# A fused time-mix, channel-mix and mixture-of-experts kernel: rank counts one step later, output projection moved, third norm and a plus-one on ScalarE

## Chip, cores and metric

One core of one Trainium2 chip. The metric is device time in microseconds of one launch, everything from the first to the last instruction; the times shown are the median of three launches.

## What is computed

The input x is 8 x 1024 tokens of 256 numbers (8192 tokens), all in float32. Cut to what matters:

```python
xn = layernorm(x)                                    # norm without gain
y  = layernorm(xn; ln1)                              # first norm of the block
r, w, k, v = sigmoid(y Wr), -exp(y Ww), y Wk, y Wv
num_t = decay*num + exp(w+k)*v;  den_t = decay*den + exp(w+k)   # scan over the 1024 tokens
xn = xn + (r * num/den) Wo
z  = layernorm(xn; ln2)
xn = xn + sigmoid(z Wrec) * (relu(z Wkey)**2) Wval   # 256 -> 1024 -> 256
x  = x + xn
h  = layernorm(x)                                    # third norm
gate = sigmoid(h Sel);  top 4 of 32 experts per token
out = x + sum over the 4 of  gate_e * relu(h K_e) V_e
```

## The kernel before

The kernel has three stages, one behind the other. The **mix stage** does everything up to the choice of experts, writes the new x to DRAM (`residual`), and scatters each token's normed row to the lists of its four experts. The **expert stage** works through 160 blocks of 256 list rows. The **combine stage** adds the four weighted expert rows to x. The change is wholly in the mix stage (`mix_phase`), so the rest is not described.

Every float32 matmul that must be exact is done as three matmuls of type fp32r on a high and a low part of both operands: high x high, high x low, low x high. So whatever goes into a matmul is first copied to a `_hi` tile (ScalarE, L588, L637, L653, L699) and then has its rest taken into a `_lo` tile (VectorE, L739, L835, L859, L912).

**Tiles and steps.** The tokens are cut in NT = 16 tiles of 512 (J = 4 subtiles of 128). There are 19 steps. In step t the engines work at the same time on tile t (time mix: projections, scan, output projection), on tile U = t-1 (channel mix) and on tile V = t-2 (third norm, routing); the scatter of rows is for tile W = t-3. Each engine has its own written-out order of work within a step, the function `step` in its block, and the engines meet only in semaphores. So a wait holds back everything behind it on the same engine. `run` (L304) unrolls the first steps, loops over pairs of steps, and unrolls the last ones.

**TensorE's order in one step**, with the lines: eight groups of six projection matmuls of tile t, m = 0 to 7 (L385), where before m = 6 come the eight transposes of the second norm of U (L375, `second_transposes`, wait for `xn2_ready` and `xn2_last_ready`); keys 0 to 3 of U, six matmuls each (L385, wait for `xn2t_ready` and `ku_ready`); the eight transposes of the third norm of V (L375, wait for `x3_ready`); keys 4 to 7; the recurrence gate of U: per subtile one bias matmul (L496, `ones_rows` times `rec_bias`, of which only two of the 64 rows, 0 and 32, are not zero) and six more (L499 to L501); the routing logits of V (L516); the transposes of the first norm of tile t+1 (L375, `t1`); 96 value matmuls of U (L535 to L539, wait for `klo_ready`); the rank counts of V, 14 small bf16 matmuls on `mask` (L554, L557); 24 matmuls of the output projection of t (L570 to L572, wait for `y_ready`).

**ScalarE's order**: u and th_r of tile t (L621, L625), second norm of U applied (L594, `xn2`, three subtiles; VectorE does the fourth, L821), the exponentials `den` (L632, wait for `ku_ready`), `xn2t_hi` (L637), then the eight keys: relu(0), relu(1), square(0), relu(2), square(1), relu(3), square(2), relu(4), x3t copies (L668), relu(5), relu(6), square(3), relu(7), square(4), first norm of t+1 applied (L594), squares 5 to 7, `th_c` (L685), `eg` (L692), `xn1t_hi` (L588), `y_hi` (L699). A square is two instructions (L652, L653).

**VectorE's order**: `xp` of U from the output projection (L800, wait for `o_ready`), statistics of the second norm (L727, L733), `th_c` and `xp` of V (L813, L817), fourth subtile of the second norm (L821), u (L827, gives `ku_ready`), statistics of the third norm, `xn2t_lo` (L835), `num` (L843), third norm of V applied (L849, gives `x3_ready`, waits for the scale from GpSimd, L1079), four scans (L868), statistics of the first norm of t+1, reciprocals and `k_lo` in turns, `xn1t_lo` (L739), routing of V (`route`: L940 adds one, L942 reciprocal, top four, `mask` at L968), `y_lo` (L912), and `route_slots`: L974 to L986, with a wait for the rank counts, and a wait for GpSimd's product L1168 (`chosen` times `place`) in the middle.

**GpSimd's order**: scale of the second norm (L1073 to L1079), x added to xp (L1141, waits for both parts of xn2), two scatters (L1124), scale of the third norm, `u` from `den` (L1148), two scatters, scale of the first norm of t+1, six scatters, `th_r` times `u` (L1158), six scatters, `chosen` times `place` (L1168). **SP** only loads x and stores xp.

Of the kernel before, what the change touches and what calls it, by code (L numbers as in the profile page):

```python
# [23 lines left out]
ALU = mybir.AluOpType  # L24
# [3 lines left out]
P = 128  # L28
# [7 lines left out]
NT = N // TILE  # L36
# [85 lines left out]
def mix_phase(nc, mix, sem, g):  # L122
# [30 lines left out]
    LO_ROW, BIAS_ROWS = 32, 64  # L153
# [119 lines left out]
    over_done, area_cleared = per("over_done area_cleared")  # L273
# [53 lines left out]
    with nc.Block() as block:  # L327
# [44 lines left out]
        def _(pe):  # L372
# [24 lines left out]
            def step(t, p, pair):  # L397
                has_t, has_u, has_v, has_next, _ = stages(t)
                U, V = t - 1, t - 2
# [21 lines left out]
                if has_t:  # L421


                    for m in range(8):
# [5 lines left out]
                        elif m in (2, 3):  # L430
                            pe.wait_ge(u_ready, 2 * t + m - 1)
# [9 lines left out]
                elif has_u:  # L441
                    second_transposes()
# [99 lines left out]
                if has_v:  # L542

                    pe.wait_ge(mask_ready, V + 1)
                    if has_next:
                        pe.wait_ge(xn1t_ready, 2 * t + 4)
                    elif has_u:
                        pe.wait_ge(xn2t_ready, 2 * U + 2)
                    else:
                        pe.wait_ge(rank_used, V)  # L550
                    for j in range(J + 1):
                        cols = ps[:, TR, j * E:(j + 1) * E]
                        for i in range(j):
                            mm = pe.matmul(cols, ones_bf[:], mask[:, i, :], start=i == 0,  # L554
                                           stop=j == J and i == j - 1)
                        if j < J:
                            mm = pe.matmul(cols, tri_bf[:], mask[:, j, :], start=j == 0, stop=True)  # L557
                    mm.then_inc(rank_ready, 1)
# [25 lines left out]
        def _(act):  # L584
# [5 lines left out]
            def ln_apply(n, dst, src, tile, ready, subtiles=J):  # L590

                act.wait_ge(rs_ready[n], tile + 1)
                for j in range(subtiles):
                    ins = act.activation(dst[:, j, :], src[:, j, :], ACT.Identity, scale=rs[:, n, j:j + 1],  # L594
# [3 lines left out]
            def step(t, p, pair):  # L598
# [64 lines left out]
                square(2)  # L663
                relu(4)
# [24 lines left out]
                if has_v:  # L689
# [3 lines left out]
                                   scale=-1.0).then_inc(eg_ready, 1)  # L693
# [25 lines left out]
        def _(dve):  # L719
# [39 lines left out]
            def step(t, p, pair):  # L759
                has_t, has_u, has_v, has_next, _ = stages(t)  # L760
                U, V = t - 1, t - 2
# [33 lines left out]
                if has_u:  # L795

                    dve.wait_ge(o_ready, U + 1)
                    landed(dve, x1_stored, p, pair, 3)
# [690 lines left out]
```

## Time and profile before

| what | value |
|---|---|
| median of three runs | 1458.73 us (1451.87 to 1459.62) |
| span of the profiled execution | 1618.1 us |
| busy: TensorE, VectorE, ScalarE, GpSimd | 1184.4, 1096.5, 678.8, 889.3 us |
| mean granted clock of TensorE | 0.862 of full speed |
| mix stage in the profile | 0 to about 880 us |

The page of the profile gives the profiled execution by its span, 1618.1 us, and has no other time for it; it is 159 us above the median of the runs that were timed without a profile. In the steady part of the mix stage (100 to 800 us) one step takes about 50 us, the granted clock is 0.97 to 1.00, and nothing in DMA is near its limit. A row of a timeline reads: start in us from the start of the span, duration in us, engine, line, operation, output and inputs, shapes, count, and in brackets how long the engine had been idle before it and what ended that.

### The profile page before, as it was taken

What the parts mean: (1) busy time and instruction counts of PE and PEld (TensorE: products, weight loads), DVE (VectorE), ACT (ScalarE), POOL (GpSimd) and SP (SyncE); (2) the same over time, 40 slices, a digit from 0 to 9 for tenths busy, and PEclk for the clock granted to TensorE, in tenths of its full rate; (3) what the DMA queues carried; (4) which work ended last, traced back from release to release, by engine and by line L of the source; (5) the groups of instructions that cost most, each with busy time, mean ns of one, the idle gap of its engine ahead of it and who ended that gap; (6) DMA issues with size and microseconds to landing.
All of it is one profiled execution on the core that took longest, in us unless ns stands there. A gap on an engine that the chain in (4) does not pass through costs nothing. (4 is left out here: it accounts for less than half of the span.)

```text
span 1618.1 us, 28319 instructions
## 1 busy us (share of the span) xinstructions
PE 1184.4 (73%) x7399; PEld 1058.3 (65%) x7400; DVE 1096.5 (68%) x2519; ACT 678.8 (42%) x1265; POOL 889.3 (55%) x967
## 2 busy tenths in 40 slices
PE   6799999999999999999881266766776766773000
PEld 5688887888878887788771266666766666673000
DVE  4889898888988889888847444444544444443987
ACT  2555565445654456444443143443443443442000
POOL 1634676666766677667657455555555555554000
PEclk9899999999999999999985588798788788886555
DMA  5000121111111121121163754445444444434998
GB/s 184 14 27 13 68 70 60 66 53 69 65 59 65 46 78 59 61 70 60 54 274 143 249 151 137 140 137 149 133 146 144 133 143 142 141 113 158 390 390 321
DMA packets 101917, 201.25 MB, mean 124 GB/s; under 512 B 16983, under 2 KB 49901, under 8 KB 100464
## 3 DMA queue, kind: packets, MB, share of 16 engines
q1 hardware_dynamic: 63216, 120.34, 23.6%
q0 software_dynamic: 27648, 67.70, 11.5%
q10 hardware_dynamic: 11008, 12.65, 2.2%
q8 instruction: 22, 0.36, 0.1%
q14 instruction: 23, 0.19, 0.0%
HBM read 105.28 MB, written 103.71 MB: 129 GB/s over the span
## 5 line engine op out<-in xcount | busy, mean ns | idle before, releaser
L1359 POOL DMA_INDIRECT expert_rows<-y,dest x320 | 320.4, 1001 | 257.1 <-issue 224.9
L1124 POOL DMA_INDIRECT lists<-rows,slot x256 | 276.5, 1080 | 73.3 <-issue 70.4
L1269 PE MATMUL ps<-xt_hi,keys 128*128 128x256 f32 x640 | 180.0, 341 | 114.0 <-issue 110.1
L1336 DVE TENSOR_TENSOR xt_lo<-ps,xt_hi 128x512 fp32r<-128x512 f32 x160 | 110.5, 690 | 186.0 <-ACT xt_hi L1296 107.6
L1269 PEld LDWEIGHTS ps<-xt_hi,keys 128*128 128x128 f32 x640 | 131.4, 226 | 130.7 <-issue 129.5
L1308 ACT ACTIVATE y<-ps 128x512 f32<-128x512 f32 x160 | 96.1, 601 | 130.2 <-PE ps L1284 113.2
L535 PE MATMUL ps<-wv_hi,k_hi 128*128 128x256 f32 x512 | 149.6, 292 | 0.0
L537 PE MATMUL ps<-wv_lo,k_hi 128*128 128x256 f32 x512 | 147.8, 289 | 0.9 <-issue 0.9
L539 PE MATMUL ps<-wv_hi,k_lo 128*128 128x256 f32 x512 | 147.6, 288 | 0.3 <-issue 0.3
L1296 ACT ACTIVATE xt_hi<-ps 128x512 fp32r<-128x512 f32 x160 | 96.6, 604 | 122.0 <-PE ps L1256 101.9
L1282 PE MATMUL ps<-experts_w,h_hi 128*128 x320 | 108.4, 339 | 47.6 <-DVE h_lo L1343 36.7
L1256 PE MATMUL ps<-consts,xr 128*128 128x128 f32 x640 | 115.3, 311 | 32.7 <-DMA xr<-lists 32.7
L1343 DVE SCALAR_TENSOR_TENSOR h_lo<-ps,h_hi 128x256 fp32r<-128x256 f32 x160 | 67.9, 424 | 93.5 <-ACT h_hi L1302 68.4
L644 ACT ACTIVATE kr<-ps,bias_k 128x512 f32<-128x512 f32 x128 | 88.2, 689 | 73.0 <-PE ps L385 70.0
L1302 ACT ACTIVATE h_hi<-ps 128x256 fp32r<-128x256 f32 x160 | 62.3, 389 | 125.6 <-PE ps L1269 87.1
L1256 PEld LDWEIGHTS ps<-consts,xr 128*128 128x128 f32 x640 | 89.2, 162 | 33.4 <-DMA xr<-lists 33.4
L1282 PEld LDWEIGHTS ps<-experts_w,h_hi 128*128 128x128 f32 x320 | 73.6, 230 | 55.6 <-issue 55.6
L385 PE MATMUL ps<-xn2t_hi,wk_hi 128*128 128x512 f32 x256 | 104.0, 406 | 1.4 <-DVE xn2t_lo L835 1.4
L385 PE MATMUL ps<-xn1t_hi,wt_hi 128*128 128x512 f32 x256 | 102.3, 400 | 2.6 <-DVE xn1t_lo L739 2.6
L1283 PE MATMUL ps<-experts_w,h_hi 128*128 x320 | 103.3, 323 | 0.0
L1284 PE MATMUL ps<-experts_w,h_lo 128*128 x320 | 102.3, 320 | 0.0
L385 PE MATMUL ps<-xn2t_lo,wk_hi 128*128 128x512 f32 x256 | 102.0, 398 | 0.0
(201 smaller groups left out, 3544.4 us busy)
## 6 DMA issues: line engine op xcount, KB each, us to landing
xr<-lists SPq DMA_DIRECT2D x160, 260.0 KB
ye<-expert_rows SPq DMA_DIRECT2D x32, 1024.0 KB, 8.1
x_sb<-in_x SPq DMA_DIRECT2D x16, 512.0 KB, 3.8
residual<-xp SPq DMA_DIRECT2D x16, 512.0 KB, 4.9
experts_raw<-in_expert_in SPq DMA_DIRECT2D x8, 1024.0 KB, 15.1
lists<-zeros SPq DMA_DIRECT2D x25, 260.0 KB, 10.8
expert_rows<-y,dest POOLq DMA_INDIRECT x320
resid<-residual SPq DMA_DIRECT2D x20, 256.0 KB, 5.4
```

Of the source, the lines that this page charges most:

```text
L385: mm = pe.matmul(bank, w(k), m(k), start=n == 0, stop=n == last)
L535: pe.matmul(bank, k_hi[:, f, c], wv_hi[:, f, :], start=f == 0 and j % 2 == 0, stop=False, skip_group_check=True)
L537: pe.matmul(bank, k_hi[:, f, c], wv_lo[:, f, :], start=False, stop=False, skip_group_check=True)
L539: mm = pe.matmul(bank, k_lo[:, f, c], wv_hi[:, f, :], start=False, stop=f == KF - 1, skip_group_check=True)
L1124: pool.indirect_dma_start(lists, bass.IndirectOffsetOnAxis(ap=slot[:, q, n:n + 1], axis=0), rows[:, q, n // TOPK, :], None).then_inc(scatt ...
L1256: mm = pe.transpose(ps[:, XT + r % 2, k * BLOCK + s * P:k * BLOCK + (s + 1) * P], xr[:, r % SLOTS, s, k * P:(k + 1) * P], ident)
L1269: mm = pe.matmul(ps[:, H + q, 0:BLOCK], keys[:, (r - 1) % SLOTS, half, k * DE:(k + 1) * DE], m[:, q, k, :], start=n == 0, stop=n == 3 * KD ...
L1282: pe.matmul(cols, h_hi[:, q, c], v_hi, start=True, stop=False)
L1283: pe.matmul(cols, h_hi[:, q, c], v_lo, start=False, stop=False)
L1284: mm = pe.matmul(cols, h_lo[:, q, c], v_hi, start=False, stop=True)
L1336: dve.tensor_tensor(xt_lo[:, q].rearrange("p k b -> p (k b)"), ps[:, XT + q, :], xt_hi[:, q].rearrange("p k b -> p (k b)").bitcast(F32), A ...
L1359: pool.indirect_dma_start(expert_rows, bass.IndirectOffsetOnAxis(ap=dest[:, r, s:s + 1], axis=0), y[:, r, s, :], None, bounds_check=OUT_RO ...
```

## The change

Four edits in the mix stage, all in the written-out orders:

1. **Rank counts a step later.** TensorE's 14 small matmuls for a tile are no longer behind the value matmuls of step t but in step t+1, between projection groups m = 1 and m = 2 (`ranks`, for tile W = t-3). On VectorE `route_slots` is cut in two: `route_places` (the old L974, L978) behind the statistics of the second norm, and the rest (the old L983, L986) behind the fourth subtile of the second norm, ahead of L827. GpSimd's product (the old L1168) moves from the end of a step to behind the scale of the second norm, ahead of L1141.
2. **Output projection straight behind the value matmuls**, which follows from 1. On VectorE `y_lo` now comes ahead of `route`.
3. **The bias matmul of 128 rows** in place of 64: `BIAS_ROWS = P`; rows other than 0 and 32 are zero as before.
4. **Third norm and plus one on ScalarE.** The four `tensor_scalar` of L849 become four activations with scale and bias, placed between square(2) and relu(4); the plus one of L940 becomes an activation behind `eg`, with a wait for it. In addition `route` waits for the scatter of the tile before last, and GpSimd waits for the last `x3_ready` before it writes the next scale.

`run` unrolls six first steps in place of four. TensorE's place for the third norm's transposes (between key 3 and key 4) is not changed.

```diff
-    LO_ROW, BIAS_ROWS = 32, 64
+    LO_ROW, BIAS_ROWS = 32, P
...
-        for t in range(4):
+        for t in range(6):
...
-        with eng.Fori(2, NT // 2 - 1) as pair:
+        with eng.Fori(3, NT // 2 - 1) as pair:
...
+                def ranks():
+                    if not has_w:
+                        return
+                    pe.wait_ge(mask_ready, W + 1)
+                    if not has_t:
+                        pe.wait_ge(xn2t_ready, 2 * min(t - 1, NT))
+                        pe.wait_ge(rank_used, W)
+                    for j in range(J + 1):
...
+                    mm.then_inc(rank_ready, 1)
...
                         elif m in (2, 3):
+                            if m == 2:
+                                ranks()
                             pe.wait_ge(u_ready, 2 * t + m - 1)
...
-                if has_v:
-
-                    pe.wait_ge(mask_ready, V + 1)
...
-                    mm.then_inc(rank_ready, 1)
...
                 square(2)
+                if has_v:
+                    landed(act, scattered, p, pair, 4, J * TOPK)
+                    ln_apply(2, rows[:, p], xp[:, p], V, x3_ready)
                 relu(4)
...
-                                   scale=-1.0).then_inc(eg_ready, 1)
+                                   scale=-1.0).then_inc(eg_exp, 1)
+                    act.wait_ge(eg_exp, V + 1)
+                    act.activation(eg[:], eg[:], ACT.Identity, bias=ones_f[:, 0:1]).then_inc(eg_ready, 1)
...
                     ln_aggr(1, U)
+                if has_w:
+                    route_places(W)
...
                                       rs[:, 1, J - 1:J], ALU.subtract, ALU.mult).then_inc(xn2_last_ready, 1)
+                if has_w:
+                    route_slots(p, pair, W)
                 if has_t:
                     for m in range(KD):
                         dve.wait_ge(u_ready, 2 * t + m + 1)
...
-                if has_v:
-                    landed(dve, scattered, p, pair, 4, J * TOPK)
-                    dve.wait_ge(rs_ready[2], V + 1)
-                    for j in range(J):
-                        ins = dve.tensor_scalar(rows[:, p, j, 0:D], xp[:, p, j, :], mv[:, 2, j, 0:1],
-                                                rs[:, 2, j:j + 1], ALU.subtract, ALU.mult)
-                    ins.then_inc(x3_ready, 1)
...
-                dve.tensor_scalar(eg[:], eg[:], 1.0, None, ALU.add).then_inc(route_step, 1)
...
+            def route_slots(p, pair, W):
+
+                dve.wait_ge(placed_ready, W + 1)
                 dve.tensor_reduce(slot_f[:], chosen[:], AX_X, ALU.add).then_inc(place_summed, 1)
-                dve.wait_ge(place_summed, V + 1)
-                landed(dve, scattered, p, pair, 4, J * TOPK)
-                dve.tensor_copy(slot[:, p, :], slot_f[:]).then_inc(slot_ready, 1)
+                dve.wait_ge(place_summed, W + 1)
+                landed(dve, scattered, p, pair, 5, J * TOPK)
+                dve.tensor_copy(slot[:, 1 - p, :], slot_f[:]).then_inc(slot_ready, 1)
...
+                if has_w:
+                    pool.wait_ge(place_ready, W + 1)
...
+                                       ALU.mult).then_inc(placed_ready, 1)
+                if has_u:
                     pool.wait_ge(xn2_ready, U + 1)
                     pool.wait_ge(xn2_last_ready, U + 1)
                     pool.tensor_tensor(xp[:, 1 - p], xp[:, 1 - p], x_sb[:, 1 - p], ALU.add).then_inc(xx_ready, 1)
                 scatter(t, 1 - p, 0, 2)
                 if has_v:
+                    if not isinstance(V, int) or V > 0:
+                        settled_on(pool, x3_ready, V)
                     ln_scale(2, V)
```

## Rows read from the trace of the kernel before

**Rows 1.** Waits of TensorE, 100 to 800 us: total us, times, longest
```profile
PE ps L375 <- ACT xn L594: 23.1, 22, 2.0
PE ps L570 <- DVE y_lo L912: 4.4, 7, 0.7
PE ps L557 <- DVE mask L968: 3.0, 6, 0.9
```

**Rows 2.** TensorE timeline, the step that begins at 401.18
```profile
401.18 0.40 PE L385 MATMUL ps<-xn1t_hi,wt_hi 128*128 128x512 f32 x1
...
410.30 1.09 PE L375 MATMUL ps<-consts,xn 128*128 128x128 f32 x8 [0.79 <-ACT xn L594]
...
414.00 0.40 PE L385 MATMUL ps<-xn2t_hi,wk_hi 128*128 128x512 f32 x1
...
419.60 1.03 PE L375 MATMUL ps<-consts,rows 128*128 128x128 f32 x8
...
426.16 0.38 PE L496 MATMUL ps<-rec_bias,ones_rows 64*128 64x256 f32 x1
...
427.37 0.38 PE L496 MATMUL ps<-rec_bias,ones_rows 64*128 64x256 f32 x1
...
433.71 1.06 PE L375 MATMUL ps<-consts,xn 128*128 128x128 f32 x8 [0.93 <-ACT xn L594]
```

**Rows 3.** TensorE timeline, the end of that step and the first matmul of the next
```profile
447.62 0.19 PE L557 MATMUL ps<-mask,tri_bf 128*128 128x32 bf16 x1
...
447.98 0.36 PE L570 MATMUL ps<-wo_hi,y_hi 128*128 128x256 f32 x1
...
452.56 0.40 PE L385 MATMUL ps<-xn1t_hi,wt_hi 128*128 128x512 f32 x1
```

**Rows 4.** ScalarE timeline, same step
```profile
421.34 0.63 ACT L653 ACTIVATE k_hi<-kr 128x512 fp32r<-128x512 f32 x1
...
431.38 2.08 ACT L594 ACTIVATE xn<-x_sb,shift_n,rs 128x256 f32<-128x256 f32 x4 [0.64 <-POOL shift_n L1107]
```

**Rows 5.** VectorE timeline, the end of that step and the start of the next
```profile
439.43 2.30 DVE L940 TENSOR_SCALAR eg<-eg 128x128 f32<-128x128 f32 x1
...
452.25 0.69 DVE L983 TENSOR_REDUCE slot_f<-chosen 128x16 f32<-128x512 f32 x1 [1.18 <-POOL chosen L1168]
...
453.09 1.66 DVE L800 SCALAR_TENSOR_TENSOR xp<-xn,ratio,ps 128x256 f32<-128x256 f32 x4
...
456.29 0.38 DVE L733 BATCH_NORM_AGGREGATE mv<-stats 128x2 f32<-128x6 f32 x4
...
457.94 1.23 DVE L817 TENSOR_TENSOR xp<-xp,th_c 128x1024 f32<-128x1024 f32 x1
...
460.94 0.69 DVE L827 TENSOR_TENSOR u<-ps,u 128x512 f32<-128x512 f32 x1 [0.67 <-PE ps L385]
...
462.91 1.29 DVE L835 TENSOR_TENSOR xn2t_lo<-ps,xn2t_hi 128x512 fp32r<-128x512 f32 x2
```

**Rows 6.** VectorE timeline, third norm in the next step
```profile
467.79 1.38 DVE L849 TENSOR_SCALAR rows<-xp,mv,rs 128x256 f32<-128x256 f32 x4 [2.01 <-POOL shift_n L1079]
```

**Rows 7.** GpSimd timeline, same stretch
```profile
439.08 2.55 POOL L1158 TENSOR_TENSOR th_r<-th_r,u 128x512 f32<-128x512 f32 x2
...
450.93 1.29 POOL L1168 TENSOR_TENSOR chosen<-chosen,place 128x512 f32<-128x512 f32 x1 [1.67 <-DVE place L974]
...
458.38 0.85 POOL L1079 TENSOR_TENSOR shift_n<-minus_mean,rs 128x4 f32<-128x4 f32 x1
460.93 2.39 POOL L1141 TENSOR_TENSOR xp<-xp,x_sb 128x1024 f32<-128x1024 f32 x1 [1.70 <-ACT xn L594]
```

**Rows 8.** VectorE timeline, the drain
```profile
840.74 0.23 DVE L940 TENSOR_SCALAR eg<-eg 128x128 f32<-128x128 f32 x1 [4.41 <-ACT eg L692]
```

**Rows 9.** TensorE timeline, the drain, after its last matmul at 803.44
```profile
812.41 1.97 PE L375 MATMUL ps<-consts,xn 128*128 128x128 f32 x8 [8.69 <-ACT xn L594]
```

**Rows 10.** Windows of 2 us: PE, PEld, DVE, ACT, POOL busy, PEclk, DMA
```profile
806.00:808.00 2.00, 0.00 (x0) 0.00 (x0) 1.93 (x8) 0.00 (x0) 0.00 (x0) 0.70 0.00 0
```

More of the change, by code:

```diff
@@ L397, in step @@
             def step(t, p, pair):
-                has_t, has_u, has_v, has_next, _ = stages(t)
-                U, V = t - 1, t - 2
+                has_t, has_u, has_v, has_next, has_w = stages(t)
+                U, V, W = t - 1, t - 2, t - 3
+                def ranks():
[6 more added lines that the diff above has]
+                    for j in range(J + 1):
+                        cols = ps[:, TR, j * E:(j + 1) * E]
+                        for i in range(j):
+                            mm = pe.matmul(cols, ones_bf[:], mask[:, i, :], start=i == 0,
+                                           stop=j == J and i == j - 1)
+                        if j < J:
+                            mm = pe.matmul(cols, tri_bf[:], mask[:, j, :], start=j == 0, stop=True)
+                    mm.then_inc(rank_ready, 1)
                 def second_transposes():
@@ L440, in step @@
                                (lambda k: xn1t_hi[:, k, :], lambda k: xn1t_lo[:, k, :]), KD, proj_ready)
-                elif has_u:
+                else:
+                    ranks()
                     second_transposes()
@@ L541, in step @@
                     mm.then_inc(val_ready, 1)
-                if has_v:
-                    pe.wait_ge(mask_ready, V + 1)
[L545 to L557, printed above, removed]
-                    mm.then_inc(rank_ready, 1)
                 if has_t:
@@ L798, in step @@
                     landed(dve, x1_stored, p, pair, 3)
+                    after(dve, x3_ready, U - 1)
                     for j in range(J):
@@ L906, in step @@
                     lo1(t + 1)
-                if has_v:
-                    route(t, p, pair, V)
                 if has_t:
@@ L929, in step, with route @@
                 if has_v:
-                    route_slots(t, p, pair, V)
-            RS = 7
-            def route(t, p, pair, V):
+                    route(p, pair, V)
+            RS = 6
+            def route(p, pair, V):
                 def after_route(n):
@@ L1137, in step @@
                         split(2, wv_hi, wv_lo, raw_v)
+                if has_w:
+                    pool.wait_ge(place_ready, W + 1)
+                    if isinstance(W, int) and W == NT - 1:
+                        pool.wait_ge(over_done, 1)
+                    pool.tensor_tensor(chosen[:].rearrange("p (j k) e -> p j k e", j=J),
+                                       chosen[:].rearrange("p (j k) e -> p j k e", j=J),
+                                       place[:].unsqueeze(2).broadcast_to([P, J, TOPK, E]),
+                                       ALU.mult).then_inc(placed_ready, 1)
+                if has_u:
                     pool.wait_ge(xn2_ready, U + 1)
@@ L1162, in step @@
                     split(0, wk_hi, wk_lo, raw_k)
-                if has_v:
-                    pool.wait_ge(place_ready, V + 1)
-                    if isinstance(t, int) and V == NT - 1:
-                        pool.wait_ge(over_done, 1)
-                    pool.tensor_tensor(chosen[:].rearrange("p (j k) e -> p j k e", j=J),
-                                       chosen[:].rearrange("p (j k) e -> p j k e", j=J),
-                                       place[:].unsqueeze(2).broadcast_to([P, J, TOPK, E]),
-                                       ALU.mult).then_inc(placed_ready, 1)
             run(pool, step)
```

37 lines of the change are left out of this document (18 added, 19 removed).

## The prediction

> **What bounds the kernel now.** I read the page first: its slices show TensorE near full in the mix stage, VectorE close behind, and DMA low. A busy share does not say who sets the pace, so next came the waits of TensorE over the steady part [rows 1]. There are 14 steps in these 700 us, and the longest entry is 23.1 us in all, 1.65 us a step. The rest is work in TensorE's own queue: it is the bound, and what lengthens or shortens that queue shows in the end nearly one for one. Then I laid out one step along TensorE's timeline [rows 2, 3]. The step begins at 401.18 (s), the second norm's transposes start at 410.30 after an idle 0.79, key 0 starts at 414.00 (K), the third norm's transposes at 419.60, the gate at 426.16, the first norm's transposes at 433.71 after an idle 0.93, the rank counts at 447.62, the output projection at 447.98, and the next step begins at 452.56: 51.4 us. All that follows asks two things of the other engines' timelines [rows 4 to 7]: when, counted from s or from K, do they hand TensorE what it waits for, and is that later than TensorE gets there?
>
> Two averages. The 0.93 recurs in each step, so of the 23.1 us about 13.0 are the first norm's and 10.1, or 0.72 a step, the second norm's. From s to K is 12.82 us here; with the mean wait in place of 0.79 it is 12.75.
>
> **Third norm on ScalarE, the largest term.** VectorE now does it in 1.38 us after a wait of 2.01 [rows 6], before key 3 is through, so TensorE goes into the transposes without idling [rows 2]. Moved, it stands on ScalarE behind square(2), whose last instruction starts at 421.34 and takes 0.63, so ScalarE is free at 421.97 [rows 4]. ScalarE has been busy without a gap since relu(1), so nothing lets it come sooner. Four activations with scale and bias of just this shape take 2.08 [rows 4], so the normed rows are there at about 424.0, and TensorE, which has not moved the transposes, has wanted them since 419.60. It stands for 4.4 us, and keys 4 to 7 stand behind it. Both ends of this count from K, so a later K doesn't soften it. **+4.4 us a step.** relu(4) is queued behind the four activations, but its key comes later than they do. The wait that this edit adds for an old scatter is met long before. What VectorE gives up, 1.38 plus the 2.01, is free, since VectorE isn't what TensorE waits for afterwards: credit zero.
>
> **Routing pieces ahead of key 0.** VectorE starts `xp` at 453.09, s + 0.53, and ends the statistics at 456.67, s + 4.1 [rows 5]. Now two small additions follow; the same size of operation took 0.23 with nothing in its way [rows 8], so 0.5 together, an estimate. `th_c` and the addition to `xp` (1.27, then 1.23, rows 5) end at s + 7.1. GpSimd's scale was held up by that addition: 0.85 for four elements, ending with it [rows 5, 7]. Its product of `chosen`, 1.29 [rows 7], also reads two tiles of SBUF, so I let it start at 7.1 and end at 8.5. VectorE waits for it, then reduces (0.69, rows 5) to about 9.3. Then comes the cast of the slots. Meanwhile GpSimd has gone on to add x to `xp`, 2.39 us [rows 7], from about 8.9 to 11.3. Does that hold the cast up? No row has a cast against it. Below, it costs nothing: reduction and cast together took 0.84 (452.25 to 453.09, rows 5). Above, the nearest row is the plus one: from float32 SBUF to SBUF, 0.23 in the drain and 2.30 in the steady step, where it ended at 441.73, just after GpSimd's products ended at 441.63 [rows 5, 7, 8]. I take it as held, until s + 11.45; free, it would be s + 9.45. A gain is excluded, as the cast is new at this place.
>
> The Trainium skill, page "SBUF — State Buffer", section "Who interferes with whom", says that copy, cast and tensor_scalar can run in a mode that takes the port pair which VectorE shares with GpSimd, for a whole instruction. By that rule the cast is held and the sum is the 1513 below; if casts of 16 elements stayed out of that mode, it would be the 1485. The trace agrees on tensor_scalar (2.30 against 0.23) and shows no cast in this position.
>
> Behind the cast stand the two subtractions of L827, 1.38 [rows 5], which before were through at 461.63. From there to the end of `xn2t_lo` at 464.20 is 2.57: ScalarE does the two exponentials first and only then the high copies. So key 0 can start at s + 11.45 + 1.38 + 2.57 = s + 15.4. TensorE gets there at s + 12.3 (12.03 without a wait, plus 0.36 for the rank counts, rows 3, now in this stretch). Against the 12.75 of before: **+2.65 us a step**; with a free cast, +0.65.
>
> **What is given back.** The bias matmul of 64 rows starts a group of seven that takes 1.21 us (426.16 to 427.37, rows 2). 24 matmuls of 512 columns took 5.60 (414.00 to 419.60), so one of 256 is worth 0.117 and seven are 0.82. I take the excess of 0.39 as the price of changing between 64 and 128 rows: four times, **-1.5 us**. At worst the excess is not from the rows and nothing is gained. The first norm's transposes, whose wait was 0.93, come 5.5 us later against K while ScalarE's application of that norm hangs on work that is no more than 2 us later: **-0.93**. The rank counts leave the end: **-0.36**; with them go the waits for the mask and `y_lo`, 7.4 us in 14 steps [rows 1], since `y_lo` is no longer behind the routing: **-0.5**. The plus one costs ScalarE some 0.3 ahead of `xn1t_hi`, which TensorE wants only a stretch of 96 value matmuls later: zero. Its 2.30 on VectorE is slack, zero. If that cover were gone it would be a gain of 2, since VectorE would have been the bound. The last tile's counts, lists and plan keep their chain, and the two more unrolled steps run the same instructions: zero.
>
> **The sum.** 4.4 + 2.65 - 1.5 - 0.93 - 0.36 - 0.5 = +3.8 us a step for the 13 steps with all four tiles in flight (3 to 15), 49 us. Step 2 has the third norm but no counts, +1.5; step 16 has no projections, and the norm, slots and bias come to about +5; step 1 only saves its bias, -1.5. Together +54. The profiled execution's span of 1618.1 would become 1672. It lies 159 us above the median, and the page doesn't say in which stage, so I carry the 54 over as microseconds: 1458.7 + 54 = **1513**.
>
> **Rivals.**
> *The cast is not held up* (for: it is 16 elements and could slip in; against: the 2.30). 14 steps lose 2.0 less each: 1485.
> *The clock falls in the new idle time.* In the drain TensorE's last matmul began at 803.44, and in the window from 806 to 808 the granted clock was already 0.70, so the engine was going to its lower level of 1.2 GHz; eight transposes then took 1.97 instead of 1.03 [rows 2, 9, 10]. Whether an idle 4.4 us does the same no row shows. If it happens each time, the transposes lose 0.94 and a key group of 1.40 costs another 1.4, 2.3 us in each of 15 steps: 1548. If in half of them, 1530. Against it: idle 0.79 and 0.93 are no measure. The Trainium skill, page "TensorE: Matmul & The Clock Gate", section "HAM oscillation — how this bites in real kernels", tells of such an alternation; the drain agrees, and by it the sum would be the 1548.
> *Faster: the end of the step gives way.* The 24 output matmuls took 4.58 us (447.98 to 452.56) for 24 x 0.117 = 2.8, and the 96 value matmuls took from about 434.5, where the transposes of 433.71 are through, to 447.6, 13.1 for 11.2. If these 3.7 us a step are only TensorE being fed late, by VectorE's full queue, then freeing VectorE gives them back, and with a free cast the step is 3.8 - 2.0 - 3.7 = 1.9 shorter: 1432. It decides where the two new waits together stay under 7.0 - 1.9 = 5.1 us a step. For it: VectorE waits little, and the change relieves it of most. Against: the waits listed for TensorE there are 0.5 us a step, and the 4.4 alone nearly fills the 5.1.
> *It cancels*: a part of that give-back, or a third norm that comes 2 us earlier than laid out, leaves it within 0.5%.
>
> **Numbers.** The case laid out, 0.50 (its own range 1500 to 1530, with the clock falling now and then); free cast 0.20; clock falling in most steps 0.17; faster 0.08; cancelled 0.05. A measurement of this kernel tells about 0.5%, 7 us, from no change, which gives faster 0.08, same 0.05, slower 0.87. The range from 1478 to 1548 takes in the first three but for the outer half of the clock case.
>
> **What would show it.** In the changed kernel: TensorE's wait for ScalarE's rows in front of the third norm's transposes, 4.4 us in 15 steps (the decisive row; were it under 2, the forecast falls). A wait of some 3 us for `xn2t_lo` in front of key 0, and the slots' cast taking about 2 us instead of 0.17. The gap from one bias matmul to the next, 0.82 instead of 1.21. No wait for the first norm's transposes, for `y_lo` or the mask. The step at about 55 us instead of 51.4.

## The result, and the profile after

The changed kernel takes 1537.06 us (median of four runs, 1534.25 to 1542.48), the kernel before on the same chip 1457.06 us (1451.87 to 1459.62). The ratio is 1.0573, with a 95% interval of 1.0547 to 1.0599: **slower by 80 us**. The forecast was 1513, in a range of 1478 to 1548.

The profiled execution of the changed kernel took 1536.0 us. The first part of its page:

```profile
span 1534.1 us, 28169 instructions
...
PE 1119.5 (73%) x7399; PEld 1005.3 (66%) x7400; DVE 1112.2 (72%) x2439; ACT 718.4 (47%) x1345; POOL 911.2 (59%) x967
```

This span can't be set against the 1618.1 of before as it stands, because the chips differ in speed. On two of the chips used later the kernel before takes about 1620 us, on the third 1453, and its first profile has a span like the slower ones. What differs most is the expert stage, which the change doesn't touch; so profiles are compared up to the first load of that stage, and times only within a chip. To that load the kernel before took 915.6 us (the "about 880" of the table ahead of the prediction stops short of it) and the changed one 977.7.

One step of the changed kernel on TensorE's timeline, the same places as in [rows 2, 3] (start, duration, engine, line, operation, in brackets the idle time before it and what ended it):

```profile
530.86 0.40 PE L385 MATMUL ps<-xn1t_hi,wt_hi 128*128 128x512 f32 x1
...
539.59 1.09 PE L375 MATMUL ps<-consts,xn 128*128 128x128 f32 x8
...
545.84 0.50 PE L385 MATMUL ps<-xn2t_hi,wk_hi 128*128 128x512 f32 x1 [2.40 <-DVE xn2t_lo L847]
...
557.46 1.97 PE L375 MATMUL ps<-consts,rows 128*128 128x128 f32 x8 [4.21 <-ACT rows L596]
...
566.78 0.28 PE L515 MATMUL ps<-rec_bias,ones_rows 128*128 128x256 f32 x1
...
567.60 0.28 PE L515 MATMUL ps<-rec_bias,ones_rows 128*128 128x256 f32 x1
...
571.77 1.07 PE L375 MATMUL ps<-consts,xn 128*128 128x128 f32 x8
...
587.07 0.40 PE L385 MATMUL ps<-xn1t_hi,wt_hi 128*128 128x512 f32 x1
```

Key 0 waits 2.40 us for `xn2t_lo`, the third norm's transposes wait 4.21 us for ScalarE's `rows`, and after that they take 1.97 us instead of 1.03. The two bias matmuls stand 0.82 apart instead of 1.21. The first norm's transposes no longer wait. The step is 56.2 us long. TensorE's waits of the changed kernel from 200 to 750 us (total, times, longest) hold nothing else; before, [rows 1], neither of the two was among them:

```profile
PE ps L375 <- ACT rows L596: 42.1, 10, 4.2
PE ps L385 <- DVE xn2t_lo L847: 23.6, 10, 2.4
```

ScalarE's timeline of the same step, to be read beside [rows 4]:

```profile
554.82 0.62 ACT L655 ACTIVATE k_hi<-kr 128x512 fp32r<-128x512 f32 x1
555.34 2.06 ACT L596 ACTIVATE rows<-xp,shift_n,rs 128x256 f32<-128x256 f32 x4
```

The normed rows are finished at 557.40, and TensorE starts at 557.46. VectorE's timeline, to be read beside [rows 5]:

```profile
537.95 1.35 DVE L831 TENSOR_SCALAR xn<-xp,mv,rs 128x256 f32<-128x256 f32 x1
539.22 0.67 DVE L988 TENSOR_REDUCE slot_f<-chosen 128x16 f32<-128x512 f32 x1
540.03 2.00 DVE L991 CAST slot<-slot_f 128x16 uint32<-128x16 f32 x1
541.94 1.28 DVE L839 TENSOR_TENSOR u<-ps,u 128x512 f32<-128x512 f32 x2
...
544.50 1.29 DVE L847 TENSOR_TENSOR xn2t_lo<-ps,xn2t_hi 128x512 fp32r<-128x512 f32 x2
```

and GpSimd's, beside [rows 7]:

```profile
537.87 1.28 POOL L1147 TENSOR_TENSOR chosen<-chosen,place 128x512 f32<-128x512 f32 x1
539.61 2.38 POOL L1154 TENSOR_TENSOR xp<-xp,x_sb 128x1024 f32<-128x1024 f32 x1 [0.46 <-ACT xn L596]
```

The 16 elements of the cast take 2.00 us, and the cast ends as GpSimd's addition to `xp` ends at 541.99. The addition had begun first.

The table lays out every kernel in the same way. It is worked out from TensorE's timelines and is the mean over the eleven steps 4 to 14, in us: from the step's start (s) to the second norm's transposes (T2), key 0, the third norm's transposes (T3), the gate, the logits, the first norm's transposes (T1), the value matmuls (V), the output projection (O), and the next step.

| kernel | step | s to T2 | to key 0 | to T3 | to gate | to logits | to T1 | to V | to O | to next |
|---|---|---|---|---|---|---|---|---|---|---|
| before | 50.86 | 9.33 | 3.69 | 5.60 | 6.56 | 4.76 | 2.79 | 1.02 | 13.27 | 3.85 |
| after | 54.42 | 8.67 | 6.16 | 10.92 | 8.38 | 3.28 | 1.70 | 0.82 | 11.60 | 2.88 |
| third norm back (e1) | 50.59 | 9.38 | 6.23 | 6.24 | 6.46 | 3.28 | 2.83 | 1.10 | 12.17 | 2.88 |
| third norm only (e2) | 52.83 | 8.24 | 3.69 | 9.97 | 8.71 | 4.76 | 1.70 | 0.83 | 11.96 | 2.95 |
| bias only (e3) | 50.99 | 9.03 | 3.70 | 5.60 | 6.46 | 3.28 | 4.35 | 1.32 | 13.30 | 3.95 |
| after again (e4) | 54.34 | 8.68 | 6.16 | 10.21 | 9.00 | 3.28 | 1.70 | 0.83 | 11.60 | 2.88 |
| filler (e5) | 52.36 | 8.68 | 6.16 | 10.71 | 6.53 | 3.28 | 1.70 | 0.83 | 11.59 | 2.88 |
| slots late (e6) | 51.14 | 8.68 | 3.66 | 10.30 | 8.21 | 3.28 | 1.70 | 0.83 | 11.59 | 2.88 |
| T3 behind key 5 (e7) | 50.23 | 8.68 | 6.16 | 11.19 | 3.91 | 3.29 | 1.70 | 0.83 | 11.60 | 2.88 |
| both repairs (e9) | 48.85 | 10.01 | 3.85 | 10.28 | 4.16 | 3.29 | 1.94 | 0.83 | 11.62 | 2.88 |
| both, norm earlier (e10) | 48.43 | 9.00 | 3.69 | 10.29 | 5.03 | 3.28 | 1.70 | 0.82 | 11.72 | 2.88 |
| norm back, slots late (e11) | 49.34 | 8.78 | 3.68 | 5.61 | 6.46 | 3.28 | 4.22 | 1.41 | 13.02 | 2.88 |

(For e7, e9 and e10 the stretch to T3 holds two keys more and that to the gate two fewer. For before, e2 and e3 the stretch from V to O also holds the 14 rank counts, 0.36 us.) From the start of step 2 to the end of step 14 the changed kernel loses 47.9 us (654.9 against 702.8), and in what is left of the mix stage 14.4. That is 62 us; the other 18 of the 80 are probably a matter of the chips, which the experiments come to.

### The profile page after: what moved, and what is told of

Same layout as the page of the kernel before. It is cut to its first block and busy times, and to the rows that moved or that the text cites. A ratio compares the mean times of both kernels' runs of the same rounds, so it can differ in the third digit from the quotient of the medians.

```text
span 1534.1 us, 28169 instructions
## 1 busy us (share of the span) xinstructions
PE 1119.5 (73%) x7399; PEld 1005.3 (66%) x7400; DVE 1112.2 (72%) x2439; ACT 718.4 (47%) x1345; POOL 911.2 (59%) x967
## 5 line engine op out<-in xcount | busy, mean ns | idle before, releaser
L1274 PE MATMUL ps<-xt_hi,keys 128*128 128x256 f32 x640 | 156.4, 307 | 78.3 <-DVE keys L1332 55.3
L864 DVE TENSOR_TENSOR k_lo<-ksq,k_hi 128x512 fp32r<-128x512 f32 x128 | 113.7, 935 | 111.1 <-ACT k_hi L655 111.1
L1274 PEld LDWEIGHTS ps<-xt_hi,keys 128*128 128x128 f32 x640 | 112.4, 194 | 100.1 <-DVE keys L1332 78.0
L385 PE MATMUL ps<-xn2t_hi,wk_hi 128*128 128x512 f32 x256 | 118.1, 461 | 33.2 <-DVE xn2t_lo L847 33.2
L1261 PE MATMUL ps<-consts,xr 128*128 128x128 f32 x640 | 98.8, 278 | 33.8 <-DMA xr<-lists 33.8
L385 PE MATMUL ps<-xn2t_hi,wk_lo 128*128 128x512 f32 x256 | 111.4, 435 | 0.0
L1332 DVE CAST keys<-experts_w 128x512 fp32r x160 | 75.1, 469 | 40.3 <-issue 37.4
L623 ACT ACTIVATE u<-ps,bias_t 128x512 f32<-128x512 f32 x32 | 22.1, 690 | 169.0 <-PE ps L385 169.0
L385 PE MATMUL ps<-xn1t_lo,wt_hi 128*128 128x512 f32 x256 | 101.0, 395 | 0.0
L385 PE MATMUL ps<-xn1t_hi,wt_lo 128*128 128x512 f32 x256 | 100.6, 393 | 0.0
```

The source lines that it names most:

```text
L385: mm = pe.matmul(bank, w(k), m(k), start=n == 0, stop=n == last)
L864: dve.tensor_tensor(k_lo[:, m, :], ksq[:, m % KRING, :], k_hi[:, m, :].bitcast(F32), ALU.subtract).then_inc(klo_ready, 1)
L1261: mm = pe.transpose(ps[:, XT + r % 2, k * BLOCK + s * P:k * BLOCK + (s + 1) * P], xr[:, r % SLOTS, s, k * P:(k + 1) * P], ident)
L1274: mm = pe.matmul(ps[:, H + q, 0:BLOCK], keys[:, (r - 1) % SLOTS, half, k * DE:(k + 1) * DE], m[:, q, k, :], start=n == 0, stop=n == 3 * KD ...
```

## The experiments

Twelve runs. e0 to e3 ran on one of the slower chips, e4 to e7 on the faster, e8 to e11 on another slower one. Each ratio is to the kernel before on the same chip.

### The kernel before and the changed kernel again (e0, e8, e4)

The kernels unchanged, one run of before at the head of each of two sets, and the changed kernel in the third.

> The kernel before unchanged, for a second profile: the profile on record lies 159 us above its median. If that was an execution with a slow expert stage, the mix stage ends at 916 us again (first load of list rows) and the span is about 1457; if the profile itself stretches this kernel, the span is 1618 again.

> The kernel before once more, for a profile where it takes about 1455 us: the profiles so far are from a chip on which it takes 1618. If only the expert stage differs between the chips, the mix stage ends at 915 us here too, and the expert stage takes about 415 us; if the chips differ in the mix stage, it ends near 898 us and the expert stage takes 430 us, as behind the changed kernel.

> The changed kernel unchanged, next to the kernel before on the same chip. In the two profiles on record its mix stage ends 62 us later (977.7 against 915.6), while its median lies 80 us higher. If the mix stage is all, the difference here is 62 us; if the expert stage also takes longer because of the change, it is 80 us again, and the first load of list rows still starts at 978.

Measured: e0 1619.81 us, e8 1621.83 us; the changed kernel 1537.48 us against 1453.15, ratio 1.0587 (1.0552 to 1.0622). The result repeats. e0 has the long span again (1617.9), but so have the runs without a profile on its chip (1620.34), so it isn't the profile that stretches the kernel. e8 was to come from a chip of the faster kind and came from another of the slower. For e4 the expectation was a difference of 62 or 80 us; it is 84. The first load of the expert stage starts at 915.42 in e0, at 914.52 in e8 and at 976.21 in e4.

The expert stage, from that load to the first load for the combine stage, took 574 us in e0 (915.42 to 1489.86) and 430 in e4 (976.21 to 1406.66). That accounts for most of the distance between the chips. If the rest of before is as long on the faster chip as that of e4 (1537.48 less 976.21 is 561 us), its mix stage ends there at 1453.15 - 561 = 892, some 23 us sooner than in its profile on a slower chip; by e7 (558 us) at 895. So the change costs about 80 us of mix stage on the faster chip, and 62 against the profile that the forecast was made from. This is an inference: before left no profile on the faster chip, and the changed kernel did not run on a slower one.

### The change without the third norm's move (e1)

```diff
                 square(2)
-                if has_v:
-                    landed(act, scattered, p, pair, 4, J * TOPK)
-                    ln_apply(2, rows[:, p], xp[:, p], V, x3_ready)
                 relu(4)
...
+                if has_v:
+                    landed(dve, scattered, p, pair, 4, J * TOPK)
+                    dve.wait_ge(rs_ready[2], V + 1)
+                    for j in range(J):
+                        ins = dve.tensor_scalar(rows[:, p, j, 0:D], xp[:, p, j, :], mv[:, 2, j, 0:1],
+                                                rs[:, 2, j:j + 1], ALU.subtract, ALU.mult)
+                    ins.then_inc(x3_ready, 1)
```

> The changed kernel with the third norm back on VectorE, behind num, as before; all else of the change stays. Theory: the wait of TensorE for the rows (4.2 us) and the two falls of the clock that go with it (12.9 us instead of 9 to 10 us from the third norm's transposes to the gate, and from key 0 to them) leave; 5.6 + 6.6 us instead of about 11 + 8.5 in 15 steps, so about 1537 - 15 x 6.5 = 1440 us, with a wait for xn2t_lo of 2.2 us still there. Rival (the load on VectorE was what mattered, and its 1.4 us plus its wait come back on the path): a gain of less than 40 us, 1500 us or more.

Measured: 1616.99 us against 1620.34, ratio 0.9991 (0.9974 to 1.0009); the first load at 912.28. Without the norm's move the whole change costs nothing. The theory had this kernel 17 us below before, the rival 43 or more above; neither came. The wait for `xn2t_lo` is there all the same, from 200 to 750 us:

```profile
PE ps L385 <- DVE xn2t_lo L844: 26.3, 11, 2.5
PE ps L375 <- ACT xn L596: 16.5, 14, 2.3
```

Key 0 starts 15.6 us behind the step's start against 13.0, the 2.6 that the forecast gave to the routing pieces; but the bias, the value matmuls and the end of the step give it back (table).

### The third norm's move alone (e2)

Before, with `ln_apply(2, ...)` on ScalarE behind square(2), the four `tensor_scalar` on VectorE gone, and the guards that go with it.

```diff
                 square(2)
+                if has_v:
+                    landed(act, scattered, p, pair, 4, J * TOPK)
+                    ln_apply(2, rows[:, p], xp[:, p], V, x3_ready)
                 relu(4)
```

> The kernel before with the third norm on ScalarE alone, at the changed kernel's place; nothing else. Theory: TensorE waits 4.3 us in 15 steps and its clock falls in them, 2 us more each: 1457 + 15 x (6.3 - 0.9) = about 1540 us, that is as slow as the whole change. Rival (the two waits add only together, since VectorE's freed time gives back at the end of the step): 1500 us or less.

Measured: 1667.19 us, ratio 1.028 (1.0261 to 1.0298), **+47 us**; the first load at 963.02, 47.6 later than e0. The theory had expected some 83 us more than before, the rival 43 or less. The wait is the one of the changed kernel to a tenth:

```profile
PE ps L375 <- ACT rows L594: 42.1, 10, 4.2
```

In the table its stretch to T3 grows by 4.37 and the next by 2.15, and the step by 1.97 only: the waits for the two other norms are gone and the value matmuls and the output projection run faster. Steps 2 to 14 lose 31 us, the rest of the stage 16. Up to the first load, e1 is 3 us shorter than e0, this run 48 longer, and the changed kernel 62 longer than before: the norm's move and the rest don't simply add.

### The bias matmul alone (e3)

```diff
-    LO_ROW, BIAS_ROWS = 32, 64
+    LO_ROW, BIAS_ROWS = 32, P
...
-                    lo_rows = slice(LO_ROW, BIAS_ROWS)
+                    lo_rows = slice(LO_ROW, 2 * LO_ROW)
```

> The kernel before with the bias matmul of 128 rows alone. Theory: 16 x 1.5 = 24 us less, 1433 us, the gap between two bias matmuls 0.82 instead of 1.21 us. Rival (what TensorE saves there it waits for behind, in front of the first norm's transposes and the counts): the gate stretch is shorter, those waits are longer, 1450 us or more.

Measured: 1623.63 us, ratio 1.0016 (1.0002 to 1.003): no gain. TensorE's timeline shows that the edit does what it should, and where it goes:

```profile
425.84 0.28 PE L496 MATMUL ps<-rec_bias,ones_rows 128*128 128x256 f32 x1
...
426.66 0.28 PE L496 MATMUL ps<-rec_bias,ones_rows 128*128 128x256 f32 x1
...
433.51 1.77 PE L375 MATMUL ps<-consts,xn 128*128 128x128 f32 x8 [2.51 <-ACT xn L594]
```

The group of seven takes 0.82 us instead of 1.21, the gate 3.28 instead of 4.76. TensorE then waits for the first norm (from 200 to 750 us; the kernel before has 20.8 in 20 there):

```profile
PE ps L375 <- ACT xn L594: 34.7, 20, 2.6
```

2.51 us in this step where [rows 2] have 0.93. The 1.5 us are handed to the next wait, as the rival said. The transposes behind it take 1.77 us instead of 1.06, and the granted clock is 0.50 from 434 to 436.

### Matmuls in the idle time (e5)

The changed kernel with 17 matmuls of 512 columns in front of the wait for the rows. Their results are overwritten by the transposes; nothing of the computation is left out.

```diff
                 if has_v:
-                    after(pe, x3_ready, V + 1)
                     if has_u:
                         pe.wait_ge(xp_ready, U + 1)
+                        for n in range(17):
+                            pe.matmul(ps[:, MISC, :], wk_hi[:, 0, 0:P], xn2t_hi[:, 0, :], start=True, stop=True)
+                    after(pe, x3_ready, V + 1)
```

> The changed kernel with 17 extra matmuls of 512 columns in TensorE's idle time ahead of the third norm's transposes, into a bank that these then overwrite; the wait itself stays. Theory (the idle time also costs clock): from the transposes to the gate 6.5 us instead of 7.8 to 9.3, about 28 to 40 us less in all. Rival (the clock falls for another reason, or what is gained is waited for later): the same time, within 10 us.

Measured: 1504.61 us, ratio 1.0355 (1.032 to 1.0391): **33 us less** than the changed kernel on that chip, with more work for TensorE and the rows no sooner. TensorE's timeline:

```profile
534.15 4.13 PE L500 MATMUL ps<-xn2t_hi,wk_hi 128*128 128x512 f32 x17
538.53 1.09 PE L375 MATMUL ps<-consts,rows 128*128 128x128 f32 x8 [0.25 <-ACT rows L598]
```

The expectation was 28 to 40 us less. With the engine kept busy the eight transposes take 1.09 us, not 1.97, and the stretch from them to the gate 6.53, not 9.00; the granted clock is 1.00 from 532 to 544. The filler brings no rows sooner, so what it saves is the clock. The granted clock of the changed kernel shows it fall (2-us windows of the step above; columns: length, busy time with count of TensorE's matmuls and weight loads, VectorE, ScalarE, GpSimd, then the granted clock, the DMA share and GB/s):

```profile
546.00:548.00 2.00, 2.00 (x6) 1.59 (x7) 2.00 (x5) 0.00 (x0) 1.82 (x3) 0.62 0.79 290
548.00:550.00 2.00, 2.00 (x6) 1.58 (x5) 2.00 (x3) 0.69 (x1) 2.00 (x2) 0.53 0.00 0
...
554.00:556.00 2.00, 0.00 (x0) 0.00 (x0) 2.00 (x1) 2.00 (x5) 1.54 (x5) 1.00 0.22 81
556.00:558.00 2.00, 0.54 (x3) 0.54 (x4) 2.00 (x3) 1.41 (x3) 1.84 (x3) 0.68 0.15 52
558.00:560.00 2.00, 2.00 (x9) 1.89 (x8) 0.74 (x2) 0.00 (x0) 1.68 (x4) 0.50 0.00 0
...
562.00:564.00 2.00, 2.00 (x7) 1.53 (x7) 0.00 (x0) 1.66 (x3) 1.57 (x2) 0.61 0.36 131
```

After the idle 2.40 and again after the idle 4.21 the granted clock goes to 0.50, the 1.2 GHz level (a window with a value between holds a change), and it is back at 1.00 within the keys that follow. The Trainium skill, page "TensorE: Matmul & The Clock Gate", section "HAM oscillation — how this bites in real kernels", tells of a kernel in which each wait for data lowers the clock for the work behind it; this trace agrees for the idle 4.21, in every step, and for the idle 2.40 in six of the steps 2 to 14.

### The slots behind `xn2t_lo` (e6)

```diff
-                if has_w:
-                    route_slots(p, pair, W)
                 if has_t:
...
                                           ALU.subtract).then_inc(xn2t_ready, 1)
+                if has_w:
+                    route_slots(p, pair, W)
```

> The changed kernel with the reduction and the cast of the slots behind xn2t_lo instead of ahead of the subtractions of L839. Theory (the cast held by GpSimd's addition is what delays key 0): the wait of 2.2 us in front of key 0 leaves, the cast takes 0.17 us, 13 x 2.2 = about 29 us less. Rival (GpSimd's product and the fourth subtile of the second norm, held by it until 9.0 us, are enough to delay key 0): under 10 us less.

Measured: 1494.65 us, ratio 1.0273 (1.0241 to 1.0305), **43 us less** than the changed kernel, where the theory had 29 and the rival under 10. The wait for `xn2t_lo` is gone, that for the rows stays:

```profile
PE ps L375 <- ACT rows L596: 49.8, 11, 4.8
```

The cast in the changed kernel (count, then duration in ns: shortest, median, longest):

```profile
L991 DVE CAST slot<-slot_f x16: 174/2084/2215, 159.8 to 944.1; 128x16 uint32<-128x16 f32 x16
```

and with the slots late:

```profile
L991 DVE CAST slot<-slot_f x16: 174/175/176, 164.1 to 900.5; 128x16 uint32<-128x16 f32 x16
```

The same 16 elements, 0.17 us with the slots late, where GpSimd is through with its addition and idle before each scatter until the slots are there, and 2.08 beside the addition to `xp`. The 43 us are more than the shift of key 0: the stretch s to key 0 gets back about 2.5 a step, the rest is the clock of the keys behind it.

### T3 behind key 5 (e7)

```diff
-                    for m in range(KF // 2):
+                    for m in range(6):
                         key(m)
...
-                    for m in range(KF // 2, KF):
+                    for m in range(6, KF):
                         key(m)
```

> The changed kernel with the third norm's transposes behind key 5 instead of behind key 3 on TensorE. Theory as first held (TensorE alone sets the pace): the wait falls from 4.2 to 1.4 us and the clock stays up, 15 x 5 = 75 us less. Theory as the bias run corrects it (the other engines need about 50 us a step, so part of what is saved comes back as waits for the first or second norm): 40 to 55 us less, with the step at 50 to 51 us and a new wait in front of the first norm's transposes.

Measured: 1472.64 us, ratio 1.0134 (1.0106 to 1.0163), **65 us less** than the changed kernel, between the two expectations. The new wait that the second expected isn't there; TensorE's list holds only these, from 200 to 750 us:

```profile
PE ps L385 <- DVE xn2t_lo L847: 25.8, 11, 2.4
PE ps L375 <- ACT rows L596: 14.7, 11, 1.3
```

Two keys are 2.8 us, and 4.2 - 2.8 is just about the 1.3 that is left. From key 0 to the gate the step takes 15.10 us instead of 19.30, so 2.87 of the 4.2 are the wait and 1.3 the clock, which now stays up through the transposes (1.09).

### Both repairs, and two variants (e9, e10, e11)

e9 is the changed kernel with the edits of e6 and e7. e10 moves the third norm in front of square(2) in addition:

```diff
                 relu(3)
-                square(2)
                 if has_v:
                     landed(act, scattered, p, pair, 4, J * TOPK)
                     ln_apply(2, rows[:, p], xp[:, p], V, x3_ready)
+                square(2)
                 relu(4)
```

e11 is e1 with the slots late, and GpSimd's third-norm scale ahead of its first two scatters:

```diff
-                scatter(t, 1 - p, 0, 2)
                 if has_v:
...
                     ln_scale(2, V)
+                scatter(t, 1 - p, 0, 2)
```

> The changed kernel with both repairs at once: slots behind xn2t_lo, and the third norm's transposes behind key 5. Theory (the two waits of the changed kernel are its whole loss, and they add): 1537 - 43 - 65 = about 1430 to 1440 us, faster than the kernel before; no wait in front of key 0. Rival (VectorE, GpSimd and ScalarE need about 50 us a step whatever TensorE does, as the bias run suggests for the old order): no better than 1460 us, with new waits for the first or second norm.

> As the run before, and ScalarE applies the third norm ahead of square(2) instead of behind it. Theory: its rows are there 1.0 us earlier, so the wait of about 1.5 us in front of the transposes shrinks to 0.5 us or goes: 8 to 15 us less than that run. Rival (the wait is too short to matter, or square(2) comes late for VectorE): the same time.

> The change without its costly part: third norm on VectorE, slots behind xn2t_lo, GpSimd's scale of the third norm ahead of the first two scatters; counts, output projection, bias and plus one as changed. Theory: neither of the two waits is there; TensorE's step is about 47 to 48 us, 1410 to 1425 us. Rival (VectorE's own queue paces the step once it has the third norm again, as in the run that put it back): 1440 us or more, with TensorE waiting for the second norm and for xn2t_lo.

Measured, against 1618.61 us: e9 1603.59, ratio 0.9913 (0.9879 to 0.9946); e10 1601.14, 0.9884 (0.9848 to 0.992); e11 1603.37, 0.9903 (0.9866 to 0.9939). All three are faster than the kernel before by about 1%, 15 to 17.5 us; their intervals overlap, so they aren't ranked. Mean steps: 48.85, 48.43 and 49.34 us. Against e8, steps 2 to 14 are 24, 29 and 19 us shorter, and the ends of the stage give 6 to 12 of that back. e9 came out as its theory had it, if that is read against the kernel before (13 to 23 us less). What TensorE waits for most in e10:

```profile
PE ps L375 <- ACT rows L596: 19.5, 12, 2.0
PE ps L385 <- ACT kr L646: 5.7, 11, 0.5
```

So e10's expectation failed: TensorE's wait for the rows is as long as in e9. ScalarE gets to them sooner but now waits for the scale, which stands on GpSimd behind two scatters, and these wait for the late slots:

```profile
602.59 2.07 ACT L596 ACTIVATE rows<-xp,shift_n,rs 128x256 f32<-128x256 f32 x4 [1.14 <-POOL shift_n L1084]
```

e10 with GpSimd's scale put ahead of those scatters, as in e11, wasn't tried. In e11 the norm is on VectorE, and the step is longer than the 47 to 48 us expected. Its wait is for the first norm; behind each of the longer ones, 2.2 to 3.2 us, the granted clock fell to 0.50, so that the value matmuls take 13.02 us instead of 11.6:

```profile
PE ps L375 <- ACT xn L596: 26.6, 15, 3.2
```

None of the three ran on the faster chip. There e6 and e7 took off 43 and 65 us of 84; whether the two together end below 1453 wasn't tried.

## Why the prediction was right, and where it was not

**The decisive row is as laid out.** Forecast: a wait of 4.4 us for ScalarE's rows. Measured: 4.21, and the time lies in the range. Counting ScalarE's queue from key 0 gave it, and e2 shows that it doesn't depend on the rest of the change.

**The cast is held**, as chosen: 2.00 us, so the case of a free cast is out. The forecast had key 0 at s + 15.4; it came at s + 14.98 in the step shown and s + 14.83 on average, 1.8 behind the 13.0 of before instead of 2.65. The product on GpSimd ended at 539.15, s + 8.3, and held up the fourth subtile on the way (L831, 1.35 us; the same operation before, L821, has a median of 0.41). By the Trainium skill, page "SBUF — State Buffer", section "Who interferes with whom", a cast can block on the port pair that VectorE shares with GpSimd, for a whole GpSimd instruction; here it agrees, at 2.00 us against 0.17.

**The step that failed: the clock was left out of the sum.** It stood only as a rival, with a chance of 0.17 and 2.3 us a step. It is the rule: from T3 to the gate each of the steps 2 to 14 takes 7.8 to 9.3 us, against 6.56 before, and from key 0 to T3 six of the thirteen take 1.5 more than the wait explains. Both together took 19.30 us against 12.16, and of the difference the wait for the rows is only 4.2; 2.9 a step is the clock. It falls behind both waits. Each repair alone keeps more than half: in e7, 15.10 - 12.16 - 1.34 leaves 1.6 for the wait of key 0, and in e6, 18.51 - 12.16 - 4.53 leaves 1.8 for the T3 wait (1.34 and 4.53 are the mean waits for the rows in these two, 14.7 and 49.8 us over 11). The argument against it, that idle times of 0.79 and 0.93 were no measure, overlooked what the trace of before shows behind the 0.93 of [rows 2] (columns as above):

```profile
432.00:434.00 2.00, 1.07 (x11) 0.99 (x11) 2.00 (x1) 2.00 (x5) 1.55 (x2) 1.00 0.18 67
434.00:436.00 2.00, 2.00 (x16) 2.00 (x14) 2.00 (x4) 2.00 (x5) 1.54 (x2) 0.69 0.35 129
436.00:438.00 2.00, 2.00 (x11) 2.00 (x11) 2.00 (x4) 2.00 (x6) 1.49 (x2) 0.50 0.20 71
```

The clock already fell there, and in six of the steps 4 to 14 the value matmuls begin at this pace, in a seventh the output matmuls run at it. Means of 0.97 to 1.00 over long slices hid it.

**The second step that failed hid the first.** "What lengthens or shortens that queue shows in the end nearly one for one": it does not. The value matmuls take 11.60 us in every step of the changed kernel, to a hundredth or two, and with the counts 12.5 to 13.7 before; the output projection 2.88 against 3.85. From V to the next step that gave back 2.6 us, where the forecast had 0.86 for the counts, the mask and `y_lo`. Laid out by the distances between TensorE's matmuls in the kernel before, the 2.6 are 0.3 for the counts, some 1.5 of waits around the counts and in the output projection, of which the forecast took 0.5 from [rows 1], and 0.75 of matmuls at the 1.2 GHz level. That TensorE was being fed late there was the mechanism of the faster rival; it holds for the waits and not for the clock, and it needed no free cast. e1 gives back 2.1 of the 2.6 with the norm still on VectorE, so most of it goes with the counts and the output projection. "Credit zero" for what VectorE gives up fails as well: in e2, where nothing but the norm moves, the value matmuls with the counts went from 13.27 to 11.96, which is full pace. Whether they profit from VectorE's shorter round or only from the time that the new wait gives every other engine, no run tells apart. So the sum of +3.8 a step against +3.56 measured is luck, errors that nearly cancel:

| term, us a step | forecast | measured |
|---|---|---|
| wait for the rows | +4.4 | +4.2 |
| start of the step to key 0 | +2.65 | +1.8 |
| clock from key 0 to the gate | 0 | +2.9 |
| bias | -1.5 | -1.5 |
| first norm's transposes | -0.93 | -1.3 |
| value matmuls to the end | -0.86 | -2.6 |
| sum | +3.8 | +3.5 |

**A saving alone is worth nothing here.** The forecast booked the bias as -1.5 in full; within this change it is right, since the two new waits made TensorE the bound. Alone (e3) it became a wait for the first norm, and e1 lost 2.6 in front of key 0 without becoming slower. This suggests that in the old order the other engines needed some 50 us for a step as well (e1 50.59, e3 50.99, before 50.86), which a list of TensorE's waits with 1.65 us a step doesn't show. It is argued from these runs and not isolated.

**The ends.** Steps 2 to 14: forecast 1.5 + 12 x 3.8 = 47, measured 47.9. The rest: forecast about 7, measured 14.4. One part is seen in the drain of the changed kernel. VectorE, GpSimd and ScalarE in turn:

```profile
913.92 8.87 DVE L758 TENSOR_TENSOR experts_w<-experts_raw,experts_w 128x2048 fp32r<-128x2048 f32 x4
```

```profile
920.59 3.09 POOL L1082 TENSOR_TENSOR rs<-ln_a,minus_half 128x4 f32<-128x4 f32 x1
923.76 0.20 POOL L1084 TENSOR_TENSOR shift_n<-minus_mean,rs 128x4 f32<-128x4 f32 x1
```

```profile
924.06 2.07 ACT L596 ACTIVATE rows<-xp,shift_n,rs 128x256 f32<-128x256 f32 x4 [6.87 <-POOL shift_n L1084]
```

With the norm off VectorE nothing holds its split of the expert weights back any more. It starts ahead of GpSimd's last third-norm scale, and GpSimd's three operations on four elements take 6.6 us (917.08 to 923.68), where for the tile before they took 1.5 (870.82 to 872.29); ScalarE sits idle for 6.87. From `place` of the last tile but one to `mask` of the last, both on VectorE, it is 29.4 us (908.43 to 937.79), and 24.0 before (850.58 to 874.54). So the "zero" of the forecast for the drain was wrong by some 5 of the 7 us, an estimate from this one place. It goes with the norm's move: behind step 14 it takes 176.2 us to the first load in e2 and 173.9 in the changed kernel, 162.5 in e1 and 159.5 before.

**The number.** 1513 was 24 us short. The mix stage was missed by 8 (54 against 62). The rest, some 16, comes from carrying microseconds of a slower chip over to a faster one, on which the kernel before seems to spend less time in the mix stage (e4, e7). The prediction said that it didn't know which stage held the 159 us; most of them are in the expert stage, but not all.

## What to carry over

Before an operation is moved to another engine, lay out when that engine gets to it and when the consumer wants it; if the consumer comes first, move the consumer's place too, as e7 does with one constant. Price a wait of some us on TensorE with the clock behind it: here that added 2.9 us to 6.6 us of waits in a step. Read the granted clock in windows of 2 us behind the waits that are there already, and not only its mean. And take a saving on one engine at its full price only where no other engine's round is as long; a warning is a stretch without listed waits that still runs slower than its matmuls can, and the short windows tell whether that is the clock or short waits.

## What was not expected of the hardware

The same kernel takes 1453 us on one chip and 1620 on two others, and the difference sits mostly in the expert stage. There SyncE computes the address of each load in registers. Its instructions of the load in the kernel before, on a slower chip (ns: shortest, median, longest):

```profile
L1240 SPq FUSED_REGOPS  x160: 3/37/711, 915.4 to 1461.9; - x160
L1240 SPq MOVE xr<-lists x160: 2/29/722, 915.5 to 1462.6; - x160
```

and in the changed kernel, on the chip where it was first measured:

```profile
L1245 SPq FUSED_REGOPS  x160: 42/42/42, 977.5 to 1374.1; - x160
L1245 SPq MOVE xr<-lists x160: 29/29/29, 977.6 to 1374.2; - x160
```

Constant to a nanosecond on the one, up to 0.7 us on the other. For MOVE all fourteen profiles sort this way: 29 ns each time in the changed kernel's and in e4 to e7, 2 or 3 to more than 700 in before and in the eight runs from the slower chips. Whether these are the cause or a sign of it stays open. For a reader of such profiles: a page and a time may come from chips that differ by 11%, and a difference in microseconds may not carry over.

Going from full rows to a bias matmul of 64 rows and back costs 0.39 us for each group of seven (1.21 against 0.82, e3), though both have 256 columns.
